# Latent keys of an attention mix spread over all 128 partitions, with a copy on the Pool engine

## What is computed

```
def _L0_xattn_ref(x, latents, mask, ...):        # x: 2 x 1024 x 256, latents: 2 x 64 x 256, 16 heads of 64
    xn = layernorm(x, ln_x_g, ln_x_b)
    ln = layernorm(latents, ln_l_g, ln_l_b)
    q = (ln @ Wq) per head
    kv = concatenate([xn @ Wkv, ln @ Wkv], axis=1)        # 1024 + 64 = 1088 keys and values
    k, v = kv per head
    qn = rmsnorm(q, qn_g) * scale ; kn = rmsnorm(k, kn_g)
    sim = qn @ kn^T, masked
    attn = softmax(sim)
    out = attn @ v
    return out @ Wout + bout
x = x + _L0_xattn_ref(ctx_1024, layernorm(x), mask, ...)
x = x + _L0_attn_ref(layernorm(x), ...)
x = x + _L0_ffn_ref(layernorm(x), ...)
```

## Time and profile before

| | us |
|---|---|
| median of 3 runs | 247.93 |
| lowest and highest | 247.34, 247.99 |
| span of the profiled execution | 245.1 |
| PE busy | 232.6 |
| DVE busy | 154.8 |
| ACT busy | 150.8 |
| POOL busy | 79.6 |

### The profile page before, as it was taken

The page is one execution under the profiler, slowest core; times in us unless marked ns, Lnnn a source line. Parts: engine busy times, 40 slices in busy tenths (PEclk is TensorE's granted clock), DMA queues, the critical chain, the costliest instruction groups (busy, mean ns, idle before and its releaser), DMA issues.

```text
span 245.1 us, 4234 instructions
## 1 busy us (share of the span) xinstructions
PE 232.6 (95%) x1509; PEld 199.7 (81%) x1509; DVE 154.8 (63%) x345; ACT 150.8 (62%) x328; POOL 79.6 (32%) x112
## 2 busy tenths in 40 slices
PE   6689999998999999999999999999999999999995
PEld 6464887876788888888888879999999888899884
DVE  1779999997687776867667655566664441303441
ACT  4354688877866768686756567777686754104141
POOL 5468776884453536464140600000000000100200
PEclk9799999999999999999999999999999999999999
DMA  5882111010000000000000899400000000000000
GB/s 180 306 276 95 47 28 38 21 45 0 21 3 0 0 4 1 0 3 0 0 3 0 261 417 322 121 3 0 0 4 0 3 1 0 3 0 0 3 0 21
DMA packets 11077, 13.67 MB, mean 56 GB/s; under 512 B 1553, under 2 KB 9777, under 8 KB 10801
## 3 DMA queue, kind: packets, MB, share of 16 engines
q1 hardware_dynamic: 10784, 12.88, 15.9%
q10 hardware_dynamic: 272, 0.52, 0.6%
HBM read 13.14 MB, written 0.13 MB: 54 GB/s over the span
## 4 chain that ended last, share of the span: by engine, by line
PE 74%; DVE 13%; DMA 3%; ACT 3%; issue 3%; POOL 2%; SPq 1%; ACTq 0%; POOLq 0%; DVEq 0%
PE banks L1103 23%; PE banks L991 13%; PE banks L1036 9%; PE banks L1065 8%; PE banks L1125 5%; PE banks L1222 4%; DVE small L761 4%; DMA rows<-in_L_xattn_ln_x_b 3%; PE banks L1118 3%; DVE sk L773 3%; PE banks L1067 3%; PE banks L1152 2%; DVE raw L729 2%; PE banks L1247 1%; DVE small L735 1%
## 5 line engine op out<-in xcount | busy, mean ns | idle before, releaser
L797 DVE TENSOR_TENSOR ptl<-banks,pth 128x512 fp32r<-128x512 f32 (+1 forms) x48 | 26.6, 555 | 32.6 <-ACT pth L562 32.0
L1103 PE MATMUL banks<-xnh,pth 128*128 128x256 f32 x128 | 37.5, 293 | 0.0
L1103 PE MATMUL banks<-xnl,pth 128*128 128x256 f32 x128 | 36.1, 282 | 0.0
L1103 PE MATMUL banks<-xnh,ptl 128*128 128x256 f32 x128 | 36.1, 282 | 0.0
L451 POOL TENSOR_TENSOR small<-small 128x16 f32<-128x16 f32 x8 | 23.3, 2907 | 35.4 <-DVE small L768 35.4
L562 ACT ACTIVATE pth<-banks 128x512 fp32r<-128x512 f32 (+1 forms) x48 | 23.6, 492 | 12.6 <-PE banks L991 10.9
L508 ACT ACTIVATE sk<-banks 128x512 f32<-128x512 f32 x36 | 20.6, 604 | 14.3 <-PE banks L1036 14.2
L413 POOL TENSOR_SCALAR tsm<-tsm 128x1 f32<-128x1 f32 x2 | 0.4, 190 | 88.8 <-DVE tsm L726 88.8
L773 DVE TENSOR_TENSOR sk<-banks,small 128x512 f32<-128x512 f32 x36 | 22.9, 678 | 7.2 <-POOL small L451 7.2
L761 DVE TENSOR_REDUCE small<-sk 128x8 f32<-128x512 f32 x36 | 23.5, 677 | 3.7 <-ACT sk L508 3.7
L1103 PEld LDWEIGHTS banks<-xnh,pth 128*128 128x128 f32 x128 | 24.4, 191 | 0.4 <-issue 0.4
(11 more groups left out here) (176 smaller groups left out, 494.1 us busy)
## 6 DMA issues: line engine op xcount, KB each, us to landing
knT<-in_L_attn_qkv_kernel SPq DMA_DIRECT2D x1, 3072.0 KB, 13.7
raw<-in_ctx SPq DMA_DIRECT2D x16, 128.0 KB, 2.0
knT<-in_L_xattn_Wq SPq DMA_DIRECT2D x1, 1024.0 KB, 9.2
wv<-in_L_xattn_Wkv SPq DMA_DIRECT2D x1, 1024.0 KB, 5.2
wout_sb<-in_L_xattn_Wout SPq DMA_DIRECT2D x1, 1024.0 KB, 5.5
knT<-in_L_attn_out_kernel SPq DMA_DIRECT2D x1, 1024.0 KB, 16.3
wraw<-in_L_xattn_Wkv ACTq DMA_DIRECT2D x1, 512.0 KB, 4.1
wraw<-in_L_xattn_Wkv SPq DMA_DIRECT2D x1, 512.0 KB, 6.4
```

The source lines that it names most:

```text
L797: nc.vector.tensor_tensor(ptl[0:rows_, j0:j1, :], banks[0:rows_, t3_bank(u, c), 0:(j1 - j0) * P].rearrange("p (j r) -> p j r", j=j1 - j0), ...
L1103: last = nc.tensor.matmul(banks[:, u_bank(u), 0:D], p_[0:r, j, :], x_, start=(j == 0 and i == 0), stop=(j == NB - 1 and i == 2))
```

## The change

The latents' block gets its 64 probabilities twice. `sp2` is 64 columns wider (1152), and POOL copies columns 1024 to 1087 of each unit to 1088 to 1151 once ACT's exponential is done (`latents_twice`, a new semaphore `twice_ready`). The block that PE transposes is then 128 wide and comes out on 128 partitions, each latent's probability once in the upper and once in the lower half. On the other side `lnh` and `lnl` become one tile `lnhl` with the high part on partitions 0 to 63 and the low part on 64 to 127. One matmul of `pth` by `lnhl` gives high by high plus high by low, a second of `ptl` by `lnhl` gives low by high (and low by low, which was left out before). The instructions of ACT and DVE on the block have 128 partitions instead of 64 and as many columns as before.

To fill `lnhl`, the normalised latents are sent to both halves of `lat2`, four transfers of 64 KB instead of two, ACT's copy writes all 128 partitions, and POOL's subtraction overwrites the lower half in place; around it POOL has two waits on its own work.

```diff
-        sp2 = sb("sp2", [P, 2, KW])
+        sp2 = sb("sp2", [P, 2, KW + M])
...
                     for b in range(B):
-                        sp.dma_start(lat64[:, b, :], lnf[b * M:(b + 1) * M, :]).then_inc(w_lat, 16)
+                        for half in range(2):
+                            sp.dma_start(lat2[half * M:(half + 1) * M, b, :], lnf[b * M:(b + 1) * M, :]).then_inc(w_lat, 16)
...
+            def latents_twice(u):
+
+                pool.wait_ge(exp_ready, u + 1)
+                nc.gpsimd.tensor_copy(sp2[:, u % 2, KW:KW + M], sp2[:, u % 2, J:KW]).then_inc(twice_ready, 1)
...
                 if i >= ITEMS_A:
                     pool.wait_ge(n2_ready, i + 1)
                     nc.gpsimd.tensor_tensor(rn[:, i % 2, :], n2[:, i % 2, :], mhalf, ALU.pow).then_inc(rnp_ready, 1)
+                    latents_twice(i - ITEMS_A)
                 if i + 1 < B * NT:
                     tile_norm(i + 1)
...
                 if i == ITEMS_A - 1:
                     pool.wait_ge(lnh_ready, 1)
-                    nc.gpsimd.tensor_tensor(lnl[:, :, :], lat64, lnh[:, :, :].bitcast(F32),
+                    pool.wait_ge(xnl_ready, i + 1)
+                    nc.gpsimd.tensor_tensor(lnhl[M:P, :, :], lat2[M:P], lnhl[M:P, :, :].bitcast(F32),
                                             ALU.subtract).then_inc(lns_ready, 1)
-
+                    pool.wait_ge(lns_ready, 1)
+
+            for u in range(ITEMS - ITEMS_A, UNITS):
+                latents_twice(u)
             pool.wait_ge(w_bout, 16)
             nc.gpsimd.tensor_tensor(xb[:, :], xb[:, :], rows[:, 2, :], ALU.add).then_inc(xb_ready, 1)
...
                 if c == 0:
                     pe.wait_ge(exp_ready, u + 1)
+                if c == 2:
+                    pe.wait_ge(twice_ready, u + 1)
...
-                transposes(banks[:, t3_bank(u, c), :], lambda i: block_of(u, j0 + i)[0], j1 - j0,
-                           width=block_of(u, j0)[1]).then_inc(pt_ps, 1)
+                transposes(banks[:, t3_bank(u, c), :], lambda i: block_of(u, j0 + i), j1 - j0).then_inc(pt_ps, 1)
...
+                        if j == NT:
+                            nc.tensor.matmul(banks[:, u_bank(u), 0:D], pth[:, j, :], lnhl[:, b, :], start=False, stop=False)
+                            last = nc.tensor.matmul(banks[:, u_bank(u), 0:D], ptl[:, j, :], lnhl[:, b, :], start=False,
+                                                    stop=True)
+                            continue
```

More of the change, by code:

```diff
@@ L72, in perceiver_layer @@
         xnl = sb("xnl", [P, B * NT, D], F32R)
-        lnh = sb("lnh", [M, B, D], F32R)
-        lnl = sb("lnl", [M, B, D], F32R)
+        lnhl = sb("lnhl", [P, B, D], F32R)
         wkh, wout_sb = shared(("wkh", [P, DC, INNER], F32R), ("wout_sb", [P, G, D], F32))
@@ L107, in early @@
             return knT[:, 1, g, at:at + width]
-        lat64 = early(0, 0, B * D)[0:M, :].rearrange("p (b d) -> p b d", b=B)
+        lat2 = early(0, 0, B * D).rearrange("p (b d) -> p b d", b=B)
         qT = early(1, 0, INNER).rearrange("p (h n) -> p h n", h=2)
@@ L222, in perceiver_layer @@
         exp_ready = sem("exp_ready")
+        twice_ready = sem("twice_ready")
         rinv_ready = sem("rinv_ready")
@@ L342, in block_of @@
         def block_of(u, j):
-            return sp2[:, u % 2, j * P:j * P + (P if j < NT else M)], (P if j < NT else M)
+            return sp2[:, u % 2, j * P:(j + 1) * P]
         T3 = [(0, 4), (4, 8), (8, NB)]
@@ L541, in exponentials @@
                 act.wait_ge(max_ready, u + 1)
-                nc.scalar.activation(sp2[:, u % 2, :], sp2[:, u % 2, :], ACT.Exp, bias=nmax[:, u:u + 1], scale=-1.0,
+                nc.scalar.activation(sp2[:, u % 2, 0:KW], sp2[:, u % 2, 0:KW], ACT.Exp, bias=nmax[:, u:u + 1], scale=-1.0,
                                      accum_out=rsum[:, u:u + 1]).then_inc(exp_ready, 1)
@@ L560, in probs_high @@
                 act.wait_ge(u_ps, u)
-                rows_ = block_of(u, j0)[1]
-                nc.scalar.activation(pth[0:rows_, j0:j1, :], banks[0:rows_, t3_bank(u, c), 0:(j1 - j0) * P].rearrange(
+                nc.scalar.activation(pth[:, j0:j1, :], banks[:, t3_bank(u, c), 0:(j1 - j0) * P].rearrange(
                     "p (j r) -> p j r", j=j1 - j0), ACT.Copy).then_inc(pth_ready, 1)
@@ L620, in _ @@
                 if i == 3:
-                    act.wait_ge(w_lat, 16 * B)
-                    nc.scalar.activation(lnh[:, :, :], lat64, ACT.Copy).then_inc(lnh_ready, 1)
+                    act.wait_ge(w_lat, 16 * 2 * B)
+                    nc.scalar.activation(lnhl[:, :, :], lat2, ACT.Copy).then_inc(lnh_ready, 1)
             keys_out(ITEMS_A - 2, 0)
@@ L783, in logits_max @@
                     dve.wait_ge(pt_ps, 3 * (u - 1))
-                nc.vector.tensor_tensor_reduce(out=sp2[:, u % 2, :], in0=logits_ps, in1=mbias[:, u // G, :], scale=-1.0,
+                nc.vector.tensor_tensor_reduce(out=sp2[:, u % 2, 0:KW], in0=logits_ps, in1=mbias[:, u // G, :], scale=-1.0,
                                                scalar=BIG, op0=ALU.add, op1=ALU.min,
@@ L794, in probs_low @@
                 j0, j1 = T3[c]
-                rows_ = block_of(u, j0)[1]
                 dve.wait_ge(pth_ready, 3 * u + c + 1)
-                nc.vector.tensor_tensor(ptl[0:rows_, j0:j1, :], banks[0:rows_, t3_bank(u, c), 0:(j1 - j0) * P].rearrange(
-                    "p (j r) -> p j r", j=j1 - j0), pth[0:rows_, j0:j1, :].bitcast(F32), ALU.subtract).then_inc(ptl_ready, 1)
+                nc.vector.tensor_tensor(ptl[:, j0:j1, :], banks[:, t3_bank(u, c), 0:(j1 - j0) * P].rearrange(
+                    "p (j r) -> p j r", j=j1 - j0), pth[:, j0:j1, :].bitcast(F32), ALU.subtract).then_inc(ptl_ready, 1)
             def unit_low(u):
@@ L1098, in mix @@
                     for j in range(j0, j1):
-                        r = block_of(u, j)[1]
-                        xh = xnh[:, b * NT + j, :] if j < NT else lnh[:, b, :]
-                        xl = xnl[:, b * NT + j, :] if j < NT else lnl[:, b, :]
+                        if j == NT:
[3 more added lines that the diff above has]
+                            continue
+                        xh = xnh[:, b * NT + j, :]
+                        xl = xnl[:, b * NT + j, :]
                         for i, (p_, x_) in enumerate(((pth, xh), (pth, xl), (ptl, xh))):
-                            last = nc.tensor.matmul(banks[:, u_bank(u), 0:D], p_[0:r, j, :], x_, start=(j == 0 and i == 0),
-                                                    stop=(j == NB - 1 and i == 2))
+                            nc.tensor.matmul(banks[:, u_bank(u), 0:D], p_[:, j, :], x_, start=(j == 0 and i == 0), stop=False)
                 if 2 in parts:
```

## The result

| | before | after |
|---|---|---|
| median, us | 247.76 | 241.53 |
| lowest and highest | 247.34, 247.99 | 240.97, 241.73 |
| span of the profiled execution | 245.1 | 239.8 |
| PE busy | 232.6 | 228.3 |
| POOL busy | 79.6 | 83.3 |

These are four runs of each on one chip. The ratio is 0.975, with a 95% interval of 0.9734 to 0.9766. The change takes 6.2 us off. I had forecast 4.8 us and a time between 241.6 and 244.8 us, so the kernel is faster, as forecast, but by more than the range allowed.

What follows compares the result with a forecast made beforehand. PE was taken as the bound (74% of the chain of waits); capped mix gains of 2.04 + 0.06 + 1.95 + 0.27 + 0 + 0.20 + 0.27 = 4.79 us, added costs 0, gave 243.1 us, range 241.6 to 244.8.

Steps and rivals of the forecast that it cites:

- The gaps belong to the shape: PE's mix: 0.28 us of longer starts around half-array matmuls vanish with 64 rows; rival that they stay, 246.2 us, chance 0.05.
- The mix gains 0.39 us: PE, last full matmul to transposes: 0.12 for the matmul gone plus 0.28 for gaps, 0.40, taken as 0.39 per mix.
- The caps: Before PE's transposes of probabilities: exponential or another wait limits gains to 0.34 in units 1, 3-7, 0.27 in 9, 0 in 8.
- No withholding: Rival: exponentials follow PE in the capped rounds, so all 16 mixes give 0.39, together 6.2, time 241.7 us; chance 0.11.
- Units 4 to 6: Exponential to transposes is 0.40 or 0.41 us, less 0.06 for the wait, so 0.34 us gained in each unit.
- Unit 2: ACT's mask row delays the exponential, so only 0.06 us can be gained before the transposes.
- Unit 15: End of the last mix: ACT waits for it with 0.27 us of idle time, so 0.27 us gained.
- The copy: POOL's 16 copies of 128 x 64: 0.3 us each, between 0.1 and 0.72, costing nothing on the path.
- scaling held up: Rival: POOL's copy holds up DVE's key scaling in rounds 1 to 7, time 245.4 or 244.4 us; chance 0.12.
- slower: Rival: POOL's copy is late for PE's transpose of the latents' block; at 4 us per copy 251.7 us; chance 0.04.
- The rest ... So 0: Outside the mixes: extra transfers and POOL's waits around the low part change nothing, 0 us.
- From span to median: Profiled span 245.1 less 4.8 is 240.3; adding the same 2.8 around it gives 243.1, against a median of 247.93.

Runs made afterwards that it cites:

- pad3: Kernel before with the latents' three matmuls on 128 rows instead of 64, lower halves zeroed once, no copy on POOL; 243.44 us, ratio 0.984.
- half2: Kernel before without the matmul of high probabilities by the latents' low part, the other two still on 64 rows; 245.42 us, ratio 0.9916.
- max_first: Changed kernel with DVE's maximum of the next unit's logits moved ahead of the low part of the latents' block; 240.23 us, ratio 0.9705.
- no_copy: Changed kernel without POOL's 16 copies and PE's wait for them, the second 64 columns zeroed once; 241.58 us, ratio 0.9768.
- a_again: Changed kernel, unchanged, run once more beside the kernel before; 241.67 us, ratio 0.9774.
- max_mask_heads: max_first with ACT's mask rows of rounds 2 and 3 ahead of the squares, heads' output copies later from unit 8; 240.46 us, ratio 0.9715.

## Where the prediction held and where it failed

**The gaps belong to the shape: held.** pad3 and half2 show it from both sides. The Trainium skill, TensorEngine Tiling (Array Packing), Key Properties, has the rule that a mode switch drains the engine; the runs agree that a switch costs time, 0.37 us to 64 rows and back; no row shows a drain as such.

**The mix gains 0.39 us: too small.** This is the term that was mis-sized. I read the gaps at the earlier trace rows, where the exit from 64 rows leads straight into transposes of probabilities, and I compared starts only up to the first of these. The exit also lengthens the instruction behind that one (0.53 instead of 0.43 us, unit 12), which lies beyond the last start that I looked at. Where nothing withholds the gain, a unit saves 0.50, and 5 x 0.39 = 1.95 became 2.45. The earlier trace rows have the places from which this could have been seen: there a matmul stands between the mix and the transposes, and the distance across it had to be compared with one where it follows a full matmul.

**The caps: right in size, in units 4 to 6 for a reason that was not the one given.** Unit 8 gave 0 (PE waits 0.25 us), unit 9 0.26 of the 0.27 forecast, and unit 7 0.35 of 0.34. There the exponential is the limit: max_first, which has it earlier, is another 0.47, 0.25 and 0.11 us shorter in units 8, 9 and 7. *No withholding* is refuted as a mechanism, although its time, 241.7, is near the one measured: the sum of 6.2 has other parts.

Units 4 to 6 gave 0.29 where I had 0.34, and here the exponential is not the limit. PE does stand 0.05 us behind it after the change, as I had said, but max_first has it earlier, and these units are as long there as in the changed kernel. Timelines at the end of unit 5, first the kernel before (L1103 is the mix, L991 the transposes), which answers to the earlier trace rows:

```profile
127.70 0.28 PE L1103 MATMUL banks<-xnh,ptl 128*128 128x256 f32 x1
...
128.25 0.28 PE L1103 MATMUL banks<-lnh,ptl 64*128 64x256 f32 x1
...
129.09 0.44 PE L991 MATMUL banks<-ident,un 128*128 128x128 f32 x2
```

the changed kernel:

```profile
126.38 0.28 PE L1121 MATMUL banks<-xnh,ptl 128*128 128x256 f32 x1
...
126.56 0.18 ACT L555 ACTIVATION_READ_ACCUMULATOR sp<-sp,small 128x1 f32 x1
126.62 0.28 PE L1115 MATMUL banks<-lnhl,ptl 128*128 128x256 f32 x1
...
126.79 0.66 PE L1002 MATMUL banks<-ident,sp 128*128 128x128 f32 x4
...
127.47 0.44 PE L1002 MATMUL banks<-ident,un 128*128 128x128 f32 x2
```

and max_first:

```profile
125.73 0.19 ACT L555 ACTIVATION_READ_ACCUMULATOR sp<-sp,small 128x1 f32 x1
...
126.13 0.28 PE L1115 MATMUL banks<-lnhl,ptl 128*128 128x256 f32 x1
...
126.98 0.44 PE L1002 MATMUL banks<-ident,un 128*128 128x128 f32 x2
```

The transposes of `un`, the mix's result, start 0.84 or 0.85 us after the last matmul of the mix in all three, whatever the exponential does. Up to them PE waits for ACT, which copies the result out of the bank (in the kernel before from 128.56 to 129.03). So a unit here saves what lies ahead of its last mix matmul, 0.12 + 0.09 + 0.10 = 0.31 us, and the two longer starts at the exit fall into a wait. In figures: from the last full matmul to `un` it is 1.39 us before and 1.09 after. pad3 confirms it. There the exponential holds nothing (0.13 us of distance), and units 4 to 6 gain 0.19 to 0.22 us and not 0.37. This chain stood in the trace of the kernel before, and the prediction has no term for it. That its limit, 0.30, lies so near to my 0.34 is luck.

Unit 2 was read wrongly too. I put its late exponential down to ACT's mask row. But round 3 has such a row as well and its distance is 0.41 us, and in round 2 ACT is idle for 0.28 us behind the row, waiting for PE. What is late is DVE's maximum, behind a pause for which the profile shows no wait. Timeline of the kernel before:

```profile
92.42 1.29 DVE L785 CUSTOM_DVE_ANT_0 sp<-banks,mbias 128x1088 f32<-128x1088 f32 x1 [0.20 <-issue]
```

The changed kernel has the same pause (0.21 us), pad3 and no_copy have none in this round. Its cause stays open. The sum of units 2 and 3 comes out all the same. In units 0 and 1, 0.45 for 0.54, PE waits 0.18 us for the second half of the scaled keys in round 1, where I had looked for it. Unit 15 gave 0.34 for 0.27.

**The copy: held.** I took 0.3 us between bounds of 0.1 and 0.72, and it is 0.24. Round 15 was the place where it could have come onto the path:

```profile
194.66 0.73 POOL L482 TENSOR_TENSOR xb<-xb,rows 128x256 f32<-128x256 f32 x1
...
196.04 0.38 PE L1214 MATMUL banks<-xb,ident 128*128 128x256 f32 x1
```

The copy of the last unit starts at 194.47, and the addition behind it ends at 195.39, 0.65 us before PE's matmul; I had 0.58. The rivals *scaling held up* and *slower* fall: DVE's scaling beside the copy still takes 1.29 us for two in round 1, as in the earlier trace rows, and no_copy is no faster. The transpose of the latents' block at 128 columns costs nothing beyond the 0.11 us between starts.

**"The rest ... So 0": failed.** This is the larger error, 0.94 us. I had the two waits around the low part before me, and asked only whether POOL would be late for its power operation. A wait also moves the instruction behind it, and here it moved it away from a DVE instruction. The evidence stood in the earlier trace rows: line 729, median 0.41 us, once 1.45. I quoted it as a warning against the copies and did not look up where the 1.45 us were, nor who waited behind them (PE, 1.05 us). The Trainium skill, GPSIMD Engine Reference, 1. Specifications, has POOL and DVE share their SBUF interfaces and names DVE instructions in a 2-port mode or with two SBUF inputs. I had used the rule against the change. The trace agrees in that the two can hold each other up; line 729 has one SBUF input, and no run shows in which mode it ran. The change ends this one costly case.

**From span to median: off by up to 1 us, without effect on the difference.** I applied the gain to the median as well as to the span, so the error falls out. It only shows that a single profiled span of this kernel can lie 1 us off before item 9's key transposes.

Put together: 4.79 forecast, plus 0.33 in the rounds (0.50 in units 10 to 14, less small losses elsewhere), plus 0.94 ahead of them, makes 6.06; measured 6.2 with an uncertainty of 0.4, and 5.8 in a_again. The range failed because its low end was set by *no withholding* with the mix's 0.39, and no case in it had a gain outside the rounds.

## What to carry to other kernels

When a gap before an instruction is to go, measure until the distances between starts are back to normal, also behind the first instruction on the far side, and at a place where no wait covers it. An outlier in a group of equal instructions (one of 1.45 us among 0.41) is a place to visit: find what runs beside it and who waits, and ask of every wait that a change adds which collisions it makes or undoes. A cap is shown only when the thing that is said to cap is moved: here the exponential was moved, and the units 4 to 6 stayed as long as they were. Once an engine is quicker, look again at the order on the engines that feed it; a swap that was worth nothing before was worth 1.3 us after.

## What the runs showed of the hardware that I had not expected

A switch of PE from 128 to 64 rows and back, with matmuls of 256 columns, lengthens four starts and not two, by 0.09, 0.10, 0.09 and 0.10 us. In the row of the first half-array matmul the load of its weights is not ahead of it: in a plain series the load starts 0.11 or 0.12 us before its own matmul (183.02 and 183.14), at the switch together with it (both at 183.35). Timeline of the kernel before, unit 12, the loads alone (PEld; their matmuls are shown above):

```profile
183.02 0.19 PEld L1103 LDWEIGHTS banks<-xnh,ptl 128*128 128x128 f32 x1
183.35 0.18 PEld L1103 LDWEIGHTS banks<-lnh,pth 64*128 64x128 f32 x1
183.46 0.19 PEld L1103 LDWEIGHTS banks<-lnl,pth 64*128 64x128 f32 x1
```

A DVE instruction with one SBUF input (128x256, float32, with two scalars) was held for the whole of a POOL subtraction when both started within 0.01 us (1.45 us beside 1.28, in the five profiles without the wait), and not at all when it was 0.2 us ahead (0.40 us, in the six with it). That is one place with two timings; how the hold depends on the offset between these was not tried. And PE's granted clock in the first 20 us differs from execution to execution, 0.83 and 0.91 in the two profiles of the kernel before, 1.00 in those of pad3, half2 and max_mask_heads. The start of item 9's key transposes, 51.48 to 52.53 us, does not follow it: 51.48 at 0.91, 52.13 at 1.00, 52.44 at 0.83.
